# A fused four-layer block on one core: ScalarE issues the small loads of its first phase, and the lists of that phase are reordered

## The reference

```
x = x + tanh(g_xattn[0]) * attention(layernorm(x), mask, ctx)            # one head, softmax(q k^T / 16 + mask) v
x = x + tanh(g_ffn[0])   * bit_ffn(layernorm(x))                         # ternary weights, tokens rounded to 8 bits
x = x + tanh(g_xattn[1]) * grouped_attention(layernorm(x), ctx)          # 16 query heads, 8 key heads, own and ctx keys
x = x + tanh(g_ffn[1])   * experts(layernorm(x))                         # 7 routed experts, top 3, and a shared one
```

## Time and profile before

| | |
|---|---|
| median of 3 runs | 596.17 us (595.9 to 598.89) |
| the profiled execution | 595.5 us |
| its span, first to last instruction | 593.8 us |
| end of the first phase in it | about 134.7 us |
| TensorE, VectorE, ScalarE, GpSimd busy | 93%, 79%, 64%, 62% of the span |

### The profile page before, as it was taken

One profiled execution on the slowest core, in us unless ns is written; L12 is line 12 of the kernel. 1 busy time (PEld: TensorE's weight loads), 2 busy tenths in 40 slices (PEclk: granted clock), 3 DMA queues, 4 the chain that ended last, 5 costly groups with the idle time before them and its releaser, 6 DMA issues.

```text
span 593.8 us, 11742 instructions
## 1 busy us (share of the span) xinstructions
PE 554.6 (93%) x4250; PEld 442.7 (75%) x4250; DVE 469.5 (79%) x972; ACT 379.6 (64%) x797; POOL 366.6 (62%) x299
## 2 busy tenths in 40 slices
PE   1998998969979999999989999999999999999996
PEld 0555444735658888888878788888888888888885
DVE  5399999787889999999999899999997754433433
ACT  1468778767876877777777877778764245343231
POOL 4031384204679878888789878787777527755231
PEclk9999999998989999999999999999999999999999
DMA  7793222115542041131482322223301001310002
GB/s 215 254 324 137 89 89 88 72 54 162 176 134 65 2 143 36 30 115 36 170 293 91 121 76 56 72 76 87 90 19 54 2 1 53 107 37 1 1 1 71
DMA packets 44569, 54.94 MB, mean 93 GB/s; under 512 B 8416, under 2 KB 30816, under 8 KB 44512
## 3 DMA queue, kind: packets, MB, share of 16 engines
q1 hardware_dynamic: 44512, 54.20, 27.9%
HBM read 41.60 MB, written 12.58 MB: 91 GB/s over the span
## 4 chain that ended last, share of the span: by engine, by line
PE 66%; DVE 4%; POOL 2%; issue 2%; ACT 1%; DVEq 0%; POOLq 0%
PE g_proj L2257 14%; PE g_proj L2345 10%; PE g_turn L2287 6%; PE g_op L2326 5%; PE g_scores L2300 5%; PE g_op L2265 3%; PE g_op L474 2%; PE g_op L475 2%; PE g_op L476 2%; PE g_proj L459 2%; PE g_proj L461 2%; PE g_proj L460 2%; PE g_turn L2309 2%; PE g_turn L459 1%; PE g_scores L459 1%
## 5 line engine op out<-in xcount | busy, mean ns | idle before, releaser
L1635 POOL TENSOR_TENSOR g_rs<-g_ve,neg_half 128x4 f32<-128x4 f32 x80 | 86.6, 1092 | 33.5 <-ACT g_ve L2007 32.6
L1656 POOL TENSOR_TENSOR g_cat<-g_yb,g_kb 128x1024 fp32r<-128x1024 bf16 x32 | 70.9, 2224 | 24.7 <-DVE g_yb L1819 24.7
L2257 PE MATMUL g_proj<-w_hi,g_xqc 128*128 128x512 f32 x192 | 84.8, 441 | 0.1
L503 POOL TENSOR_TENSOR m_h_lo<-m_h,m_h_hi 128x512 fp32r<-128x512 f32 x32 | 41.5, 1295 | 57.8 <-ACT m_h_hi L490 57.8
L2257 PE MATMUL g_proj<-w_lo,g_xqc 128*128 128x512 f32 x192 | 76.2, 397 | 0.0
L2033 ACT ACTIVATE g_qn<-g_proj,g_rs 128x128 f32<-128x128 f32 x192 | 54.9, 372 | 22.7 <-POOL g_rs L1635 12.6
L1763 DVE BATCH_NORM_STATS2 g_stats<-g_proj 128x6 f32<-128x256 f32 x160 | 60.3, 419 | 8.9 <-PE g_proj L2257 7.7
L2287 PE MATMUL g_turn<-ident,g_qn 128*128 128x128 f32 x384 | 57.4, 278 | 6.1 <-ACT g_qn L2033 6.1
L2287 PEld LDWEIGHTS g_turn<-ident,g_qn 128*128 128x128 f32 x384 | 44.2, 141 | 13.1 <-ACT g_qn L2033 6.7
L490 ACT ACTIVATE m_h_hi<-m_h 128x512 fp32r<-128x512 f32 x32 | 20.3, 633 | 49.2 <-DVE m_h L497 49.2
L1323 PE MATMUL f_bank<-f_w_ctx,f_ctxT 128*128 128x512 f32 x96 | 44.1, 592 | 0.0
(11 more groups left out here) (242 smaller groups left out, 1638.5 us busy)
## 6 DMA issues: line engine op xcount, KB each, us to landing
kvx_rows<-f_kept SPq DMA_DIRECT2D x24, 256.0 KB, 2.4
g_ksq<-kvx_rows SPq DMA_DIRECT2D x8, 512.0 KB, 4.6
g_kraw<-kvx_rows SPq DMA_DIRECT2D x16, 256.0 KB, 3.2
g_v<-kvx_rows SPq DMA_DIRECT2D x8, 512.0 KB, 4.1
m_raw<-in_L_W SPq DMA_DIRECT2D x16, 256.0 KB, 3.3
c_raw<-in_L_wqT SPq DMA_DIRECT2D x4, 512.0 KB, 5.7
f_w_ctx<-in_L_wkvxT SPq DMA_DIRECT2D x4, 512.0 KB, 7.3
c_praw<-in_L_wprojT SPq DMA_DIRECT2D x4, 512.0 KB, 5.5
```

Source lines behind the costliest of these rows:

```text
L1635: G.tensor_tensor(rs[:, at % NORMS, :], ve[:, at % NORMS, :], k["half"][:, 0:4], ALU.pow).then_inc(q["rs_done"], 1)
L1656: G.tensor_tensor(cat[:, h].rearrange("p h (b s) -> p b h s", b=2), yb[:, h, :].rearrange("p (b h s) -> p b h s", b=2, s=SEQ), kb[:, h, :] ...
L2257: last = T.matmul(bank(n, i)[:], xqc[:, n % 2, view * KT + c_, :], w[:, c_, :], start=c_ == 0 and part == 0, stop=c_ == KT - 1 and part == 1)
```

## The change

SP keeps the large loads, in another sequence; 25 small loads are issued by ScalarE, 19 of them before anything else in its list and six between its later steps. `tern.on_sync` is split, so that each ternary weight has a place of its own. GpSimd sets all constants before its first power. On every engine steps of the front change places. Amount and form of the computing, the waits inside each step and all tiles stay as they are, and the second phase is untouched.

```
@@ SP
             sp.dma_start(k['x'][:, 0:ST, :], source[:, 0:ST, :]).then_inc(x_loaded[0], 16)
+            sp.dma_start(wq[:], t['L0_WqT'].rearrange('(c p) f -> p c f', p=P)).then_inc(q['qk_loaded'], 16)
+            sp.dma_start(wk[:], t['L0_WkT'].rearrange('(c p) f -> p c f', p=P)).then_inc(q['qk_loaded'], 16)
             weights.load(sp, t, 0)
+            sp.dma_start(wv[:], t['L0_WvT'].rearrange('(c p) f -> p c f', p=P)).then_inc(q['v_loaded'], 16)
+            sp.dma_start(mask[:], t['mask'].rearrange('(n p) s -> p n s', p=P)).then_inc(q['v_loaded'], 16)
+            sp.dma_start(k['x'][:, ST:TILES, :], source[:, ST:TILES, :]).then_inc(x_loaded[1], 16)
             weights.load(sp, t, 1)
...
             weights.load(sp, t, 2)
-            sp.dma_start(k['x'][:, ST:TILES, :], source[:, ST:TILES, :]).then_inc(x_loaded[1], 16)
-            tern.on_sync(sp, t)
-            weights.load_small(sp, t)
...
+            tern.load(sp, t, 0)
+            tern.load(sp, t, 1)
+            tern.load(sp, t, 2)
             weights.load(sp, t, 3)
+            sp.dma_start(ctxT[:], t['ctxT'].rearrange('(c p) n -> p c n', p=P)).then_inc(q['ctx_loaded'], 16)
...
@@ ScalarE
+            act.dma_start(gate_raw[:, 0:2], t['g_xattn'].rearrange('(o n) -> o n', o=1).broadcast_to([P, 2])).then_inc(q['gate_loaded'], 16)
+            act.dma_start(lw[:], t['L1_ln_w']).then_inc(q['ln_loaded'], 16)
+            act.dma_start(gate_raw[:, 2:4], t['g_ffn'].rearrange('(o n) -> o n', o=1).broadcast_to([P, 2])).then_inc(q['gate_loaded'], 16)
+            act.dma_start(bv[:], t['L0_bv'].rearrange('(o n) -> o n', o=1).broadcast_to([P, E])).then_inc(q['v_loaded'], 16)
+            act.dma_start(bq[:], t['L0_bq']).then_inc(q['qk_loaded'], 16)
+            act.dma_start(bk[:], t['L0_bk']).then_inc(q['qk_loaded'], 16)
+            weights.load_small(act, t)
             act.wait_ge(q['consts_made'], 7)
             keep_tokens(0)
+            act.dma_start(lb[:], t['L1_ln_b']).then_inc(q['ln_loaded'], 16)
+            act.dma_start(ins[:, 0:KT], t['L1_q_in_scale']).then_inc(q['ln_loaded'], 16)
             act.wait_ge(q['qk_loaded'], 64)
...
             exponent(1)
-            weights.high(act, 0)
-            weights.high(act, 1)
             keep_probs(1)
             tern.scale(act, 1)
             keep_integers(0)
+            keep_context(0)
+            weights.high(act, 0)
             tern.scale(act, 2)
...
@@ VectorE, ternary layer
             hidden(1, 3)
             hidden_largest(0, 2)
+            context_mean(1)
             hidden(1, 4)
+            hidden(1, 5)
+            weights.low(dve, 2)
             hidden_largest(0, 3)
-            weights.low(dve, 2)
-            hidden(1, 5)
             hidden(1, 6)
...
@@ TensorE, tail of the front
             context(17)
+            down(0, 0)
             context(18)
-            down(0, 0)
```

More of the change, by code:

```diff
@@ L571, in __init__, with load @@
         self.clipped, self.rounded = take("tern_clipped"), take("tern_rounded")
[L573 to L576, removed]
+    def load(self, sp, t, n):
+        src, slices = (("L0_gateT", KT), ("L0_upT", KT), ("L0_downT", INNER // P))[n]
+        sp.dma_start(self.raw[n][:].rearrange("p (c f) -> p c f", c=slices),
+                     t[src].rearrange("(c p) f -> p c f", p=P)).then_inc(self.loaded[n], 16)
     def column_sum(self, act, n):
@@ L715, in _ @@
[L715 to L720, removed]
@@ L730, in _ @@
             sp.dma_start(w_ctx[:, 0], t['L1_wkvxT'][:, 0 * CH:1 * CH].rearrange('(c p) f -> p c f', p=P)).then_inc(q[f'wctx_loaded{0}'], 16)
-            for n in range(4, len(weights.kinds)):
-                weights.load(sp, t, n)
-            sp.dma_start(ctxT[:], t['ctxT'].rearrange('(c p) n -> p c n', p=P)).then_inc(q['ctx_loaded'], 16)
+            weights.load(sp, t, 4)
+            weights.load(sp, t, 5)
+            weights.load(sp, t, 6)
+            weights.load(sp, t, 7)
             sp.dma_start(w_ctx[:, 3], t['L1_wkvxT'][:, 3 * CH:4 * CH].rearrange('(c p) f -> p c f', p=P)).then_inc(q[f'wctx_loaded{3}'], 16)
@@ L930, in _ @@
             ln.apply(dve, 1, lambda j: an[:, 1, j, :])
+            weights.mean(dve, 0)
+            weights.mean(dve, 1)
             dve.wait_ge(q['v_loaded'], 48)
@@ L950, in _ @@
             divide(1)
+            product_scales(0)
             add_attention(1)
+            tern.clip(dve, 0)
             tern.clip(dve, 1)
-            product_scales(0)
             ln.moments(dve, 3)
@@ L968, in _ @@
             hidden(0, 5)
-            context_mean(1)
+            weights.mean(dve, 5)
             hidden(0, 6)
+            hidden(0, 7)
             hidden_largest(0, 0)
-            hidden(0, 7)
             tern.clip(dve, 2)
             hidden(1, 0)
+            hidden(1, 1)
             hidden_largest(0, 1)
-            hidden(1, 1)
             mean_square(0)
             hidden(1, 2)
-            weights.mean(dve, 5)
             hidden(1, 3)
             hidden_largest(0, 2)
+            context_mean(1)
             hidden(1, 4)
+            hidden(1, 5)
+            weights.low(dve, 2)
             hidden_largest(0, 3)
-            weights.low(dve, 2)
-            hidden(1, 5)
             hidden(1, 6)
@@ L1008, in _ @@
             round_hidden(1, 2)
+            weights.low(dve, 5)
             round_hidden(1, 3)
-            weights.low(dve, 5)
             round_two(0)
@@ L1128, in _ @@
             gated(0, 3)
-            weights.high(act, 2)
             keep_context(4)
+            act.dma_start(ins[:, 3 * KT:4 * KT], t['L1_qx_in_scale']).then_inc(q['ln_loaded'], 16)
             gated(0, 4)
+            keep_integers(1)
+            square(0, 1)
             gated(0, 5)
+            gated(0, 6)
             keep_context(5)
-            square(0, 1)
-            gated(0, 6)
+            square(0, 2)
+            gated(0, 7)
             keep_context(6)
-            square(0, 2)
-            keep_integers(1)
-            gated(0, 7)
             keep_context(7)
@@ L1142, in _ @@
             square(0, 3)
+            gated(1, 1)
             keep_context(8)
+            square(1, 0)
             keep_context(9)
-            gated(1, 1)
             gated(1, 2)
-            square(1, 0)
             gated(1, 3)
+            weights.high(act, 2)
             keep_context(10)
             gated(1, 4)
+            gated(1, 5)
             square(1, 1)
+            weights.high(act, 3)
             keep_context(11)
-            gated(1, 5)
             keep_context(12)
             gated(1, 6)
-            weights.high(act, 3)
             gated(1, 7)
@@ L1191, in _ @@
             over_scale(7)
+            weights.high(act, 7)
             weigh_tokens(1)
@@ L1353, in _ @@
             context(1)
+            context(2)
             gate_up(0, 0)
-            context(2)
+            gate_up(0, 1)
             context(3)
-            gate_up(0, 1)
             context(4)
@@ L1401, in _ @@
             down(1, 0)
+            down(1, 1)
             turn_hidden(1, 2)
             context(21)
-            down(1, 1)
             turn_hidden(1, 3)
```

57 lines of the change are left out of this document (24 added, 33 removed).

## The result

The changed kernel takes 600.25 us (median, 597.58 to 603.44) beside 596.32 us for the kernel before (595.67 to 598.89): ratio 1.0054, 95% interval 1.0038 to 1.0069. It is slower by 2.3 to 4.1 us, about 3.2; 593.2 was forecast. At a mean granted TensorE clock of 0.99 the executions of the kernel before take 595.0 to 597.6 us and those of the changed one 597.6 to 599.0, at 0.985 to 0.987 they take 598.2 to 599.3 and 599.7 to 602.1, so a median also depends on how many there are of each. The profiled execution of after is 3.1 us longer in its span than that of before (596.9 against 593.8), both at 0.99.

The account below looks back on a forecast made before the run. TensorE (93% busy) and VectorE (79%) leave no large hole; the front depends on the first projection's start and VectorE's density. 2.57 + 0.4 = 3.0 us off gives median 593.2, range 589.5 to 602.5.

Parts of the forecast that it names:

- So at SP's price the issues are just hidden by the loads and the layernorm, with 0.1 us to spare: Start of the front: 19 ScalarE issues at 0.50 us end at 10.3, ScalarE being wanted at 10.40.
- 15 of the 16 rows nearest in kind: Ground for 0.50 us per ScalarE issue: SP's small issues, one after another, between 21.43 and 28.96 us.
- the issues hold each other: Rival, start of the front: two engines issuing at once stop each other; slower, 602 us, chance 0.28.
- if only short stops are shared (0.8 each) it is 599: Mildest case of the slower rival: ScalarE's issues share only short stops, 0.8 us each, giving 599 us.
- 0.80 us per issue: Price of a ScalarE issue from which the slower rival decides; the kernel is then 3 us slower at the start.
- The start: Up to the first projection: normalising takes 1.38 instead of 3.83 us without GpSimd beside it; 2.57 us earlier.
- I take it as landing early enough: Second half of x, seventh instead of sixteenth on SP's queue, lands in time to hide the moved weight sums.
- would cost the whole gain: Bound if x's second half lands no sooner: sums done at 27.2 against 24.7 us.
- The middle: 27.3 to 60 us: reordered steps gain 0.4 us, bounds 0 and VectorE's idle 1.74.
- 60 to 98: Stretch of the front where GpSimd holds VectorE; taken as 0, bounds 3.7 us gained or as much lost.
- the tail: 98 to 134.7 us: moved products and weight passes are hidden in idle time; 0, give or take 1 us.
- Worth 0: Large loads on SP land earlier as its 7.22 us stop goes, but TensorE was not waiting for them; no gain.

Follow-up runs that it names:

- SP silent: Changed kernel, but the sync engine waits behind its first load until ScalarE's thirteen last small loads have landed; nineteen ScalarE issues took 9.25 us, whole time not meaningful.
- thirteen on SP: Changed kernel, but thirteen of the nineteen small loads issued by SP again, ahead of chunk 3; six stay at ScalarE's head; 596.37 us, ratio 0.9984.
- SP alone: Changed kernel's lists and sequence of large loads, but every small load issued by SP and none by ScalarE; 593.95 us, ratio 0.9941.

## Why the prediction was wrong

**The step that failed** is "So at SP's price the issues are just hidden by the loads and the layernorm, with 0.1 us to spare": I took 0.50 us an issue because "15 of the 16 rows nearest in kind" had it. Those rows are of an engine that issues alone, and alone ScalarE does pay 0.49 (SP silent). Beside SP it paid 0.81, and the table load came 4.09 us later for it. The rest of that sum was right: nineteen issues of 0.81 from 0.81 end at 16.2, 3.2 us past before's 12.97, and 3.30 was measured. The rows that I left out stood in the same trace: SP's first nineteen issues, in the same stretch of time and with the large transfers under way, took 0.70 each, above the 0.64 at which the gain is gone by my own sum. The rival "the issues hold each other" had the case in its mildest form, "if only short stops are shared (0.8 each) it is 599"; I gave it 0.28 and 602 (slower in all 0.29), and had put "0.80 us per issue" as the point from which it decides. That 600.25 lies inside 589.5 to 602.5 is owed to the width left for this rival, not to the sum. The share is partial: at 3.36 both engines stop for 1.5 us, but five issues of ScalarE pass while SP stands still for 6.94. The Trainium skill's "Perfetto Trace Analysis", section "DMA Instruction — HWDGE (DVE, Sync)", with its lock for exclusive use, agrees with the first row and not, as a rule for the whole stop, with the second.

**A term that was missing.** The sum kept x's first half where it was, so that the layernorm started as before. It landed 1.66 us later. In after this is hidden behind the issues; with six issues (thirteen on SP) it costs 1.59. I priced the issues on the engine and not what a second queue does to the transfers of the first. The Trainium skill's "DMA: Bandwidth & Descriptors", section "Issuing engines are not separate DMA queues", says that issuing on several engines saves only the time of the sequencer, and that the transfers share the same 16 engines; the runs go further, the transfers nearly stood still for a time.

**The start, -2.57 forecast.** Right in mechanism and nearly in size: -2.38 with SP alone (10.59 for 12.97). Normalising took 1.38 in every kernel with the new lists. Of the 0.19 that is missing 0.16 is the turns: the tiles are released 1.20 behind the last normalising (10.59 for 9.39) instead of 1.04.

**x's second half.** "I take it as landing early enough" held with the new sequence (14.09, 15.14 in after), and the bound "would cost the whole gain" held without it (18.94).

**The middle, 60 to 98, and the tail.** -0.4, 0 and 0 were forecast. From the first projection to the second phase it is -0.38 in after and -0.58 with SP alone (118.66 for 119.24), and 0.2 to 0.3 longer behind it. The agreement with -0.4 is partly luck, as the inner moves cancel: TensorE lost small waits, and got one of 2.17 us for `f_h` ahead of 101.75, where before waited 1.15 for it.

**"Worth 0" for the large loads on SP.** Half right: they land earlier than they are needed, but SP's long stop didn't vanish as I had it, it stays behind the ternary weights, now on the load of chunk 3 (6.94 at 13.43).

What the lists and the sequence were forecast to give, 593.2, is what they give without ScalarE's issues: 593.95. What stays open is why the engines stand still about 2.3 us after a second queue begins, whether the small loads at its head have a part in it, how the 0.81 divides between company and large transfers, and what decides whether TensorE's clock falls after the new wait.

## What to carry to other kernels

An issue has two prices: its time on the issuing engine's list, which went from 0.49 alone to 0.81 us beside another engine's issues and large transfers, and what it does to the transfers that are under way; count both up to the first instruction that waits. So the load on which the start hangs goes out with no other queue beginning beside it, and small loads go to a second engine only behind that and into waits that it has anyway, after asking who waits for them (1 KB issued at 7.8 landed at 16.1 here). A one-time cost such as the 1.28 us table load can be drawn into the wait for the first data by one idle instruction.

## What the runs showed of the hardware that was not expected

- A single 128 KB load on a second queue, issued at the same instant as x's first half, delayed its landing from 4.83 to 7.18 us; five loads of 1 KB, to 6.41; nineteen small ones, with nothing large behind x, to 5.59.
- When the second queue began at 0.80 or at 2.78 us, the rate of all 16 engines fell 2.2 to 2.4 us later, to 62 GB/s and to 2 GB/s, for some 2 us with loads outstanding. When it began at 4.7 to 5.0, no such deep hole followed at that distance, but from 10.4 to 12.4 us the rate was 154 to 170 GB/s in three kernels, with the engines 0.55 busy, against 342 with SP alone.
- The same 2.16 us wait of TensorE is followed by 1.2 GHz in some executions and by the full clock in others; eight 128x512 products take 5.19 or 3.67 us.
